# Loads of samples and stores of results issued as two transfers each, 80 rows and the rest

## The chip, the cores and the metric

One Trainium2 chip, one core of it. The metric is device time of one execution in microseconds (us), the median over runs; lower is better.

## The reference

The input x holds 64 samples of 750 time steps with 32 features. Cut to what matters here:

```python
h = tok(x, tok_W, tok_b)          # 92 patches of 16 steps, stride 8, each (512 values) @ W.T + b -> 128
h = h + attn(layernorm(h), ...)   # 8 heads of 64, softmax, heads mixed by an 8x8 matrix, layer norm over heads, values, w_out
h = h + ffn(layernorm(h), ...)    # 8 experts, the top 2 of a softmax gate, and one shared expert
return h                          # (64, 92, 128) float32
```

Everything is float32. The change touches only how x comes in and how h goes out; the arithmetic stays.

## The kernel before, in words

The 64 samples are worked on in 16 groups of 4 (SLOTS = 4, NG = 16). A sample is seen as 93 rows (NP2) of 256 values: one row is one stride of 8 steps times 32 features, and patch p is rows p and p + 1. So a group's samples are one DRAM view of 93 rows x 4 samples x 256 float32 (1 KB contiguous each), and are loaded into the buffer xin, one row of the view per SBUF partition. A group's result is 92 rows (N, the patches) x 4 samples x 128 float32 (512 bytes each), staged in the buffer ostage.

The five engines each run the same hand-written list of steps (`SETUP`, then `ORDER_0`, `STEPS` in a hardware loop, then `TAIL`), each doing its own part of a step and waiting on semaphores for the others. All DMA transfers are issued by SyncE (SP), in its program order, onto one hardware queue:

- first the identity matrix (`ident`), then, once GpSimd has cleared xin, the load of group 0 (`load(0)`, L442);
- then seven transfers counted by `first_loaded` (L467): the token weights tok_W into tok_nat (an alias of the buffer ex, so the trace says ex), biases into vecs, the gate weights;
- then qkv (L468), fifteen constants counted by `consts_loaded` (L470: lng, w_out, lnb, rev, three copies of b2, eight pieces of mixw), and four transfers of expert weights counted by `experts_loaded` (L471 to L474, into an alias of act);
- then `load(G + 2)` each time the step XO of group G + 1 has read xin (so at most one load is under way), and one store in each step OT (L482) once ScalarE has written ostage (L692). At the end SP waits for all stores.

What TensorE does at the start, in the order of `SETUP_START`: step XE (4 transposes of xin; waits for `x_loaded`), XO (4 more), pT (4 transposes of tok_W; waits for all of `first_loaded`), pB (vecs and gate), TK (12 matmuls of 368 columns, the patch embedding; needs xe, xo and the split tok weights), pA0 (waits for qkv), TH, pA1, and VectorE's prepW (L818: waits for qkv and all of `consts_loaded`, then runs L821). Later come pV, pO and, last in the setup, prepE on GpSimd, which waits for the expert weights.

`x_loaded` is counted in units of 16 for each transfer: XE of group g waits for 16 * g + 16 (L591). ScalarE waits with `at_least(act, stored, 16 * g)` before it overwrites ostage for group g, so one store is under way at a time.

Of the kernel before, what the change touches and what calls it, by code (L numbers as in the profile page):

```python
# [16 lines left out]
N = (T - PATCH) // STRIDE + 1  # L17
HEADS, DH = 8, 64
E = 8
SLOTS = 4  # L20
NG = B // SLOTS
# [3 lines left out]
NP2 = N + 1  # L25
# [5 lines left out]
LN_EPS = 1e-5  # L31
N_ROUTE = 18
COPY = 32
COPIES = 3
ROWS_CT = (COPIES - 1) * COPY + E

# [128 lines left out]
def audio_tower(nc, x, tok_W, tok_b, w_qkv, reattn_w, ln_g, ln_b, w_out, b_out, gate_w, w1, b1, w2, b2,  # L165
                sw1, sb1, sw2, sb2, ident_dram, rev_dram, out):
    with ExitStack() as ctx:
# [25 lines left out]
        gate_nat = sb("gate_nat", [E, 128])  # L193
        b2_sb = sb("b2_sb", [2 * COPY + E, 128])
        lng = sb("lng", [128, HEADS])
# [20 lines left out]
        xin = sb("xin", [NS, SLOTS, PAIRS])  # L216
# [62 lines left out]
        ostage = sb("ostage", [N, SLOTS, 128])  # L279
# [11 lines left out]
        x_loaded = sem("x_loaded")  # L291
        stored = sem("stored")
# [48 lines left out]
        def at_least(eng, s, value):  # L341

            if isinstance(value, int) and value <= 0:
                return
            eng.wait_ge(s, value)
# [86 lines left out]
        x_pairs = x_rows[:, 0:NP2 * PAIRS].rearrange("b (p k) -> p b k", p=NP2)  # L432
        out_rows = out.rearrange("b p d -> p b d")
# [5 lines left out]
        @block.sync  # L439
        def _(sp):  # L440
            def load(g):
                sp.dma_start(xin[0:NP2, :, :], x_pairs[:, bass.ds(SLOTS * g, SLOTS), :]).then_inc(x_loaded, 16)  # L442

            first = [
                (tok_nat[:, :, :], tok_W.rearrange("d (k f) -> d k f", k=KT)),
                (vecs[0:8, :], b1), (vecs[8:9, :], sb1.unsqueeze(0)), (vecs[9:10, :], sb2.unsqueeze(0)),
                (vecs[10:11, :], tok_b.unsqueeze(0)), (vecs[11:12, :], b_out.unsqueeze(0)),
                (gate_nat[:, :], gate_w),
            ]
            consts = [  # L450
                (lng[:, :], bass.AP(tensor=ln_g.tensor, offset=0, ap=[[0, 128], [1, HEADS]])),
                (wo_nat[:, :, :], w_out.rearrange("d (k f) -> d k f", k=4)),
                (lnb[:, :], bass.AP(tensor=ln_b.tensor, offset=0, ap=[[0, 128], [1, HEADS]])),
                (rev[:, :, :], rev_dram),
            ]
            for r in range(COPIES):
                consts.append((b2_sb[COPY * r:COPY * r + E, :], b2))

            for h in range(HEADS):
                consts.append((mixw[IC * h:IC * h + IC, :],  # L460
                               bass.AP(tensor=reattn_w.tensor, offset=HEADS * h, ap=[[0, IC], [1, HEADS]])))
            assert len(first) == N_FIRST and len(consts) == N_CONSTS
            sp.dma_start(ident[:, :], ident_dram).then_inc(ident_loaded, 16)
            sp.wait_ge(xin_cleared, 1)
            load(0)
            for dst, src in first:
                sp.dma_start(dst, src).then_inc(first_loaded, 16)  # L467
            sp.dma_start(qkv[:, :, :], w_qkv.rearrange("(c p) d -> p c d", p=128)).then_inc(qkv_loaded, 16)  # L468
            for dst, src in consts:
                sp.dma_start(dst, src).then_inc(consts_loaded, 16)  # L470
            sp.dma_start(w1_sb[:, 0:E, :], w1.rearrange("e h f -> h e f")).then_inc(experts_loaded, 16)  # L471
            sp.dma_start(w1_sb[:, E, :], sw1).then_inc(experts_loaded, 16)
            sp.dma_start(w2_sb[:, 0:E, :], w2.rearrange("e f h -> f e h")).then_inc(experts_loaded, 16)
            sp.dma_start(w2_sb[:, E, :], sw2).then_inc(experts_loaded, 16)  # L474

            def do(step, G):
                if step == "XO" and exists(G + 2, NG):
                    wait_filled(sp, "XO", G)
                    load(G + 2)
                if step == "OT":  # L480
                    wait_emptied(sp, "OT", G)
                    sp.dma_start(out_rows[:, bass.ds(SLOTS * (G - 2), SLOTS), :],  # L482
                                 ostage[:, :, :]).then_inc(stored, 16)

            run(sp, do)
            sp.wait_ge(stored, 16 * NG)

        @block.tensor
        def _(pe):
# [79 lines left out]
            def do(step, G):  # L569
# [11 lines left out]
                g = G + LAG[step]  # L581
# [5 lines left out]
                if step == "XE":  # L587
                    if isinstance(G, int) and G == FIRST:
                        pe.wait_ge(pool_consts, 1)
                        pe.wait_ge(ident_loaded, 16)  # L590
                    pe.wait_ge(x_loaded, 16 * g + 16)  # L591
                if step == "BS":
                    pe.wait_ge(xsum_ready, g + 1)
                if step == "OP":
# [26 lines left out]
                elif step == "TK":  # L621

                    for k in range(KT):
                        rows = [m[:, :, k // 2:k // 2 + N] for m in (xe, xo)[k % 2]]
# [64 lines left out]
        def _(act):  # L689
# [43 lines left out]
            def do(step, G):  # L733
                if isinstance(step, tuple):
                    kind, s = step
                    b = SLOTS * G + s - BEHIND[kind]
                    if kind in ("exa", "exb"):
                        softmax_exp(b, s, int(kind == "exb"))
                    if kind == "ev":
                        act.wait_ge(av_ready, b + 1)  # L740
                        act.activation(oT[0][:, :, (s - 2) % SLOTS, :], values(), ACT.Copy).then_inc(oT_high, 1)
                    if kind == "sq":
                        square(b)
                    if kind == "rstd":
                        attention_rstd(b)
                    return
                g = G + LAG[step]
                if step == "R2":
                    act.wait_ge(route, N_ROUTE * g + 2)
                    act.activation(exl[:, :, :], shift_l[:, :, :], ACT.Exp).then_inc(exl_ready, 1)  # L750
                if step[0] == "H":

                    k = int(step[1])
                    last = f"C{2 * k + 1}" if k < E // 2 else f"Z{E}"
                    wait_emptied(act, last, G)
                    two = slice(2 * k, min(2 * k + 2, E + 1))
                    act.activation(act1_split[0][:, two, :], act1[:, two, :], ACT.Copy).then_inc(units_high, 1)  # L757
                if step in NO_FILL:
                    return
                ps = bank(step)  # L760
                if step in ("XE", "XO"):
                    wait_filled(act, step, G)
                    act.activation((xe if step == "XE" else xo)[0][:, :, :], patches(ps), ACT.Copy)\
                       .then_inc(patch_high, 1)
                elif step == "TK":
                    at_least(act, shifted, G + 1)
                    empty(step, G, hT[:, :, :].rearrange("p s n -> p (s n)"), ps[:, 0:W], func=ACT.Identity,
                          bias=vecT[:, 10:11])
                elif step == "TX":
                    wait_filled(act, step, G)  # L770
                    act.activation(xT_split[0][:, :], ps[:, 0:W], ACT.Copy).then_inc(high_ready[0], 1)  # L771
                elif step == "TX2":
                    wait_filled(act, step, G)
                    act.activation(x2T[0][:, :], ps[:, 0:W], ACT.Copy).then_inc(high_ready[1], 1)
                elif step == "CT":
                    wait_filled(act, step, G)
                    act.activation(combT[0:ROWS_CT, :], ps[0:ROWS_CT, 0:W], ACT.Copy).then_inc(high_ready[2], 1)
                elif step in ("Y0", "Y2", "Y4", "Y6"):
                    empty(step, G, yT[:, :, :, int(step[1]), :], chunked(ps))
                elif step in ("V0", "V2", "V3"):  # L780
                    empty(step, G, v_sb[:, int(step[1]), :], ps[0:N, :])
                elif step[0] == "Z":
                    e = int(step[1])
                    if e == 0:
                        at_least(act, pool_units, len(UNITS_BY_POOL) * g)
                        at_least(act, dve_units, len(UNITS_BY_DVE) * g)
                        if present("YF", G - 1):
                            wait_filled(act, "YF", G - 1)
                    wait_filled(act, step, G)
                    ins = act.activation(act1[:, e, :], ps[:, 0:W], ACT.Relu, bias=vecT[:, e:e + 1])  # L790
                    ins.then_inc(emptied[BANK[step]], 1)
                elif step == "OT":
                    at_least(act, stored, 16 * g)
                    empty(step, G, ostage[:, :, :].rearrange("p s n -> p (s n)"), ps[0:N, :])

            run(act, do, prepare)
# [365 lines left out]
```

## Time and profile before

| what | value |
|---|---|
| time, median of 3 runs | 754.84 us (751.76 to 755.04) |
| the profiled execution: its own time | 750.55 us |
| the profiled execution: span of the trace | 748.8 us |
| mean granted TensorE clock | 0.972 |
| TensorE matmul busy | 685.5 us (92% of the span) |
| VectorE, ScalarE, GpSimd busy | 539.1, 469.1, 352.4 us |
| DMA | 12.03 MB, mean 16 GB/s |
| chain that ended last | PE 78%, DVE 11%, ACT 4%, DMA 1% |

The span runs from the first to the last instruction of the trace; the execution's own time is 1.75 us longer. The profiled execution was 4.29 us below the median of the runs shown. TensorE is busy nearly all the time except in the first and the last of the 40 slices of the span.

### The profile page before, as it was taken

The page shows a single profiled execution, that of the slowest core. Times are in us where ns is not written, and L with a number is a line of the kernel's source. Part 1 is how long each engine was busy: PE and PEld are TensorE (multiplying, and loading weights), DVE is VectorE, ACT ScalarE, POOL GpSimd, SP SyncE. Part 2 cuts the span into 40 slices and gives each one's busy share as a digit, 9 for nine tenths or more (in the row PEclk, how much of TensorE's full clock was granted, in tenths as well). Part 3 has the DMA queues.
Part 4 walks back from the last instruction along what each step waited for, and adds up shares of the span by engine and source line. Part 5 has one row for each costly group of instructions (what it writes and reads, how often), then busy time and mean ns, then how long its engine had stood idle before and what let it go on. Part 6 is the DMA issues. An engine that isn't in the chain of part 4 may idle for free.

```text
span 748.8 us, 16667 instructions
## 1 busy us (share of the span) xinstructions
PE 685.5 (92%) x5238; PEld 620.4 (83%) x5238; DVE 539.1 (72%) x1575; ACT 469.1 (63%) x1494; POOL 352.4 (47%) x435
## 2 busy tenths in 40 slices
PE   2679999999999999999999999999999999998846
PEld 2568889898898989898898989898898989886735
DVE  1755586968777786968777786968777786966544
ACT  1246576685848666685847666685847676675514
POOL 1434336554554536554554536554554536554302
PEclk9899899999999999999999999999999999998968
DMA  3300000000000000000000000000000000000000
GB/s 96 83 22 1 22 3 21 12 17 8 7 19 10 20 10 20 10 17 8 7 19 10 20 10 20 10 16 9 6 20 10 20 10 1 12 1 11 1 10 11
DMA packets 17057, 12.03 MB, mean 16 GB/s; under 512 B 924, under 2 KB 16776, under 8 KB 17032
## 3 DMA queue, kind: packets, MB, share of 16 engines
q1 hardware_dynamic: 17032, 11.71, 5.6%
q8 instruction: 13, 0.21, 0.1%
q14 instruction: 12, 0.10, 0.0%
HBM read 8.70 MB, written 3.01 MB: 16 GB/s over the span
## 4 chain that ended last, share of the span: by engine, by line
PE 78%; DVE 11%; ACT 4%; issue 3%; DMA 1%; POOL 1%; POOLq 0%; DVEq 0%; ACTq 0%
PE ps_fill L337 15%; PE ps_fill L339 13%; PE ps_fill L338 12%; PE ps_dots L542 11%; PE ps_mix L554 11%; PE ps_fill L497 7%; PE ps_av L562 5%; PE ps_fill L664 3%; DMA xin<-in_x 1%; DVE key L937 1%; ACT ex L701 1%; ACT xT_split_hi L771 1%; DVE xT_split_lo L1032 1%; DVE top L939 1%; DVE combine L943 1%
## 5 line engine op out<-in xcount | busy, mean ns | idle before, releaser
L1100 POOL TENSOR_TENSOR sum<-sq 92x384 f32<-92x384 f32 x64 | 64.1, 1001 | 201.7 <-ACT sq L709 201.7
L701 ACT ACTIVATE ex<-ps_dots,negmax 128x92 f32<-128x92 f32 x384 | 123.5, 342 | 38.1 <-DVE negmax L952 38.1
L542 PE MATMUL ps_dots<-xT,yT 128*128 128x96 f32 x768 | 96.4, 275 | 7.6 <-ACT ex L701 4.3
L542 PEld LDWEIGHTS ps_dots<-xT,yT 128*128 128x128 f32 x768 | 91.6, 192 | 11.3 <-issue 10.9
L554 PE MATMUL ps_mix<-mixk,probs 128*92 128x128 f32 x768 | 96.8, 277 | 2.6 <-POOL probs L1094 1.5
L1094 POOL TENSOR_TENSOR probs<-ex,rinv 128x552 f32<-128x552 f32 x64 | 71.0, 1109 | 52.6 <-DVE rinv L958 52.6
L1050 DVE TENSOR_TENSOR act<-ps_fill,act 128x368 f32<-128x368 f32 x128 | 64.5, 534 | 40.7 <-PE ps_fill L664 40.3
L790 ACT ACTIVATE act<-ps_fill,vecT 128x368 f32<-128x368 f32 x144 | 76.5, 566 | 27.3 <-PE ps_fill L339 27.0
L407 POOL TENSOR_TENSOR act_split_lo<-act,act_split_hi 128x736 fp32r<-128x736 f32 (+1 forms) x48 | 81.2, 1706 | 25.0 <-ACT act_split_hi L757 23.8
L554 PEld LDWEIGHTS ps_mix<-mixk,probs 128*92 128x92 f32 x768 | 89.5, 163 | 4.0 <-POOL probs L1094 2.0
L701 ACT ACTIVATION_READ_ACCUMULATOR ex<-ps_dots,negmax 128x1 f32 x384 | 81.6, 212 | 0.0
L971 DVE TENSOR_TENSOR aT<-ps_mix,arstd 92x360 f32<-92x360 f32 x128 | 61.6, 522 | 5.6 <-ACT arstd L719 5.0
L562 PE MATMUL ps_av<-aT,v_sb 92*64 92x96 f32 x1024 | 57.7, 256 | 3.8 <-DVE aT L973 2.3
L709 ACT ACTIVATE sq<-ps_mix 92x768 f32<-92x768 f32 x64 | 52.3, 817 | 10.0 <-PE ps_mix L554 9.9
L757 ACT ACTIVATE act_split_hi<-act 128x736 fp32r<-128x736 f32 (+1 forms) x80 | 57.1, 752 | 0.9 <-DVE act L1050 0.8
L562 PEld LDWEIGHTS ps_av<-aT,v_sb 92*64 92x64 f32 x1024 | 45.5, 139 | 13.6 <-issue 11.1
L337 PE MATMUL ps_fill<-x2T_hi,w_split_hi 128*128 128x368 f32 x144 | 51.7, 359 | 0.7 <-DVE combT L1044 0.7
L407 DVE TENSOR_TENSOR act_split_lo<-act,act_split_hi 128x736 fp32r<-128x736 f32 x32 | 47.9, 1528 | 5.9 <-ACT act_split_hi L757 5.7
L715 ACT ACTIVATE lnvar<-sumsq,eps 92x96 f32<-92x96 f32 x64 | 24.1, 376 | 42.4 <-POOL sumsq L1107 42.3
L337 PE MATMUL ps_fill<-xT_split_hi,A_hi 128*128 128x368 f32 x128 | 47.2, 368 | 3.0 <-DVE yT L802 2.3
L952 DVE TENSOR_REDUCE negmax<-ps_dots 128x6 f32<-128x552 f32 x64 | 46.3, 723 | 3.0 <-PE ps_dots L542 2.9
L337 PE MATMUL ps_fill<-act_split_hi,w_split_hi 128*128 128x368 f32 x144 | 48.4, 336 | 0.0
(169 smaller groups left out, 1772.4 us busy)
## 6 DMA issues: line engine op xcount, KB each, us to landing
xin<-in_x SPq DMA_DIRECT2D x16, 372.0 KB
out<-ostage SPq DMA_DIRECT2D x16, 184.0 KB
act<-in_L_ffn_w SPq DMA_DIRECT2D x2, 512.0 KB, 4.5
qkv<-in_L_attn_w_qkv SPq DMA_DIRECT2D x1, 768.0 KB, 8.1
ex<-in_L_tok_W SPq DMA_DIRECT2D x1, 256.0 KB
ex<-in_L_attn_w_out SPq DMA_DIRECT2D x1, 256.0 KB
mixw<-in_L_attn_reattn_w SPq DMA_DIRECT2D x8, 0.5 KB
act<-in_L_ffn_sw SPq DMA_DIRECT2D x2, 64.0 KB, 4.3
```

The source lines that it names most:

```text
L337: nc.tensor.matmul(out, s_hi, m_hi, start=start, stop=False)
L338: nc.tensor.matmul(out, s_hi, m_lo, start=False, stop=False)
L339: return nc.tensor.matmul(out, s_lo, m_hi, start=False, stop=stop)
L407: eng.tensor_tensor(lo, act1[:, two, :], hi.bitcast(F32), ALU.subtract).then_inc(done, 1)
L542: last = pe.matmul(ps_dots[:, c // HALF, o:o + NS], yT[:, 2 * s + c // HALF, c % HALF, :, :].rearrange("p h i -> p (h i)"), xT[:, N * s:N ...
L554: last = pe.matmul(ps_mix[0:N, c // HALF, o:o + 128], probs[:, (s - 1) % 2, c, :], mixk[:, :, :].rearrange("p g i -> p (g i)"), start=True ...
L562: last = pe.matmul(ps_av[o:o + DH, NS * (g // 2):NS * (g // 2) + NS], v_sb[:, (s - 2) % SLOTS, DH * g:DH * g + DH], aT[:, s % 2, N * g:N * ...
L701: last = act.activation(ex[:, s % 2, c, :], ps_dots[:, c // HALF, o:o + N], ACT.Exp, bias=negmax[:, c:c + 1], accum_out=sums[:, s % 2, c:c ...
L790: ins = act.activation(act1[:, e, :], ps[:, 0:W], ACT.Relu, bias=vecT[:, e:e + 1])
L1050: ins = dve.tensor_tensor(act1[:, e, :], ps[:, 0:W], act1[:, e, :], ALU.mult)
L1094: pool.tensor_tensor(probs[:, s % 2, :, :], ex[:, s % 2, :, :], rinv[:, s % 2, :].unsqueeze(2).broadcast_to([128, CHUNKS, N]), ALU.mult).t ...
L1100: pool.tensor_tensor(sum4[:, :, :, :], sq[:, :, 0:4, :], sq[:, :, 4:8, :], ALU.add)\
```

## The change

Each load of samples becomes two transfers, rows 0 to 79 and rows 80 to 92 of the same view; each store becomes two, rows 0 to 79 and 80 to 91. Both transfers of a pair add 16 to the same semaphore, so what waits for them counts in units of 32.

```diff
+SPREAD_ROWS = 80
...
             def load(g):
-                sp.dma_start(xin[0:NP2, :, :], x_pairs[:, bass.ds(SLOTS * g, SLOTS), :]).then_inc(x_loaded, 16)
+                for rows in (slice(0, SPREAD_ROWS), slice(SPREAD_ROWS, NP2)):
+                    sp.dma_start(xin[rows, :, :], x_pairs[rows, bass.ds(SLOTS * g, SLOTS), :]).then_inc(x_loaded, 16)
...
                 if step == "OT":
                     wait_emptied(sp, "OT", G)
-                    sp.dma_start(out_rows[:, bass.ds(SLOTS * (G - 2), SLOTS), :],
-                                 ostage[:, :, :]).then_inc(stored, 16)
+                    for rows in (slice(0, SPREAD_ROWS), slice(SPREAD_ROWS, N)):
+                        sp.dma_start(out_rows[rows, bass.ds(SLOTS * (G - 2), SLOTS), :],
+                                     ostage[rows, :, :]).then_inc(stored, 16)
...
-            sp.wait_ge(stored, 16 * NG)
+            sp.wait_ge(stored, 32 * NG)
...
-                    pe.wait_ge(x_loaded, 16 * g + 16)
+                    pe.wait_ge(x_loaded, 32 * g + 32)
...
-                    at_least(act, stored, 16 * g)
+                    at_least(act, stored, 32 * g)
```

## Rows read from the trace of the kernel before

**Rows 1.** The page: granted TensorE clock in tenths, 40 slices of the span

```profile
PEclk9899899999999999999999999999999999998968
```

**Rows 2.** Chain that ended last, in order of time: start, length, what

```profile
1.72 10.76 DMA xin<-in_x
...
12.61 2.38 PE ps_fill L497 x12
```

**Rows 3.** Timeline of the first 40 us: start, length, engine, line, what

```profile
1.72 0.31 SPq L442 DMA_DIRECT2D xin<-in_x  x1
2.08 2.02 SPq L467 DMA_DIRECT2D ex<-in_L_tok_W  x1
...
4.14 1.50 SPq L467 DMA_DIRECT2D vecs<-in_L_ffn_b  x1
...
6.86 0.27 SPq L467 DMA_DIRECT2D gate_nat<-in_L_ffn_gate_w  x1
7.18 0.40 SPq L468 DMA_DIRECT2D qkv<-in_L_attn_w_qkv  x1
7.62 3.51 SPq L470 DMA_DIRECT2D lng<-in_L_attn_ln_g  x1
...
13.76 0.82 PEld L497 LDWEIGHTS ps_fill<-ident,ex 128*128 128x128 f32 x4
...
14.04 3.55 SPq L470 DMA_DIRECT2D mixw<-in_L_attn_reattn_w  x8
...
17.63 0.42 SPq L471 DMA_DIRECT2D act<-in_L_ffn_w  x1
...
20.37 1.46 PEld L523 LDWEIGHTS ps_fill<-qkv 64*128 64x128 f32 x8 [0.41 <-issue]
...
25.08 1.38 DVE L821 TENSOR_TENSOR probs<-qkv,lng 64x512 f32<-64x512 f32 x2
```

**Rows 4.** The page's DMA issues: transfers, KB each, median us from issue to landing

```profile
qkv<-in_L_attn_w_qkv SPq DMA_DIRECT2D x1, 768.0 KB, 8.1
...
ident<-const_ident SPq DMA_DIRECT2D x1, 64.0 KB, 1.9
```

**Rows 5.** Stretches of 1 us while load 0 and the weights come in; last two columns: DMA share, GB/s

```profile
3.00:4.00 1.00, 0.00 (x0) 0.00 (x0) 0.00 (x0) 0.00 (x0) 0.76 (x7) 1.00 0.23 12
...
5.00:6.00 1.00, 0.00 (x0) 0.00 (x0) 0.00 (x0) 0.00 (x0) 0.00 (x0) 1.00 0.75 241
...
7.00:8.00 1.00, 0.00 (x0) 0.00 (x0) 0.00 (x0) 0.00 (x0) 0.00 (x0) 1.00 0.21 68
...
20.00:21.00 1.00, 1.00 (x5) 0.63 (x4) 0.00 (x0) 0.46 (x1) 0.00 (x0) 1.00 1.14 345
```

**Rows 6.** The same for a load alone (first and last of 7 rows, and one between)

```profile
44.00:45.00 1.00, 0.00 (x0) 0.00 (x0) 0.81 (x2) 0.60 (x4) 0.00 (x0) 1.00 0.14 25
...
48.00:49.00 1.00, 1.00 (x11) 1.00 (x10) 0.73 (x1) 0.08 (x1) 0.42 (x1) 1.00 0.22 74
...
50.00:51.00 1.00, 1.00 (x8) 1.00 (x7) 0.00 (x0) 1.00 (x4) 0.25 (x1) 1.00 0.14 45
```

**Rows 7.** The same for the last store (last two of 3 rows)

```profile
746.00:747.00 1.00, 0.00 (x0) 0.00 (x0) 0.00 (x0) 0.00 (x0) 0.00 (x0) 0.50 0.27 76
747.00:748.00 1.00, 0.00 (x0) 0.00 (x0) 0.00 (x0) 0.00 (x0) 0.00 (x0) 0.50 0.24 73
```

**Rows 8.** Waits of the DMA queue's engine SP: us in total, times, longest

```profile
SPq L167 <- DMA out<-ostage: 3.5, 1, 3.5
```

**Rows 9.** SP's timeline in the loop

```profile
161.63 0.27 SPq L442 DMA_DIRECT2D xin<-in_x  x1
...
203.76 0.25 SPq L442 DMA_DIRECT2D xin<-in_x  x1
```

**Rows 10.** Stretches of 2 us where the clock fell; the third last column is the clock

```profile
76.00:78.00 2.00, 1.05 (x14) 1.08 (x16) 1.47 (x4) 0.00 (x0) 0.04 (x1) 0.51 0.04 8
...
82.00:84.00 2.00, 2.00 (x14) 2.00 (x14) 0.65 (x2) 2.00 (x13) 0.00 (x0) 0.78 0.14 34
```

## The prediction

> **What bounds the kernel now.** I read the views from the whole to the place of the change. The page says TensorE is busy 92% of the span, at full granted clock in most slices [rows 1], and the chain that ended last is 78% TensorE and 1% DMA. So in the loop the transfers can matter little, and the question is whether the 1% is a place where nothing else covers them. The chain in order of time [rows 2] shows it: from 1.72 to 12.48 us it consists of one transfer, load 0, and TensorE's first work (12 transposes: XE, XO, pT) starts at 12.61. The view of SP's waits shows the second place: at the very end SP sits 3.5 us on the last store [rows 8]. Everything between is covered: in the loop SP issues one load per iteration of 203.76 - 161.63 = 42.13 us [rows 9], just after XO has read xin, and the next XE comes most of an iteration later; ostage has the same slack.
>
> **How wide a transfer is now.** A load with nothing beside it (load 2) moves its 372 KB between about 44.3 and 50.7 us; inside that stretch the mean busy share of the 16 DMA engines is 0.22, at 74 GB/s, and over its seven rows it is 1.29 engine-spans, that is 20.6 engine-us [rows 6]. 0.22 x 16 is 3.5, near three engines for 93 rows. The store shows 0.27 and 0.24, four engines, at 73 to 76 GB/s [rows 7], for 92 rows. While 128-row transfers come in, the share is 0.75 to 1.14 at 241 to 345 GB/s [rows 5]. The numbers fit equal shares: 93 = 3 x 31 on 3 engines, 92 = 4 x 23 on 4, 128 = 16 x 8 on 16. With the same reading 80 rows = 16 x 5 use all 16, the remaining 13 and 12 rows use 13 and 12.
>
> The Trainium skill says this as a rule (DMA: Bandwidth & Descriptors, "Why a DMA increments its semaphore by 16 and not by 1"): the number of engines is the largest up to 16 that divides the slowest dimension. By that rule too it is 3 and 4 now and 16, 13 and 12 after; the trace agrees, with its shares of 0.22 and 0.24 to 0.27.
>
> **The change, step 1: the transfer itself.** A load is 372 packets of 1 KB (93 rows x 4), 124 on each of 3 engines; 20.6 engine-us / 372 = 55 ns each. After, an engine has at most 5 x 4 + 4 = 24: 1.3 us where it was 6.4 to 6.9. A store is 368 packets of 512 bytes, 92 on each of 4 engines; 188 kB at 76 and 73 GB/s is 2.5 us, or 27 ns each, 30 ns with the ragged first row. After: 24 x 30 = 0.7 us. Both rates are within what 16 engines have shown (381 kB in 1.3 us is 293 GB/s, 188 kB in 0.7 us is 269, against 345 [rows 5]).
>
> **Step 2: the extra instruction.** SP issues one more transfer per load and store, 0.25 to 0.31 us each [rows 3, 9]. In the loop SP is idle between issues, so it costs nothing; if every one of the 32 lay on the path it would be 32 x 0.28 = 9 us, but then SP would have to be the one that is waited for, and it issues for about 0.5 us in an iteration of 42.13. At the start it delays what is queued behind load 0 by 0.3 us; at the end it overlaps the first part's transfer.
>
> **Step 3: the start.** XE alone isn't what counts: pT waits for all seven `first_loaded` transfers, which stand behind load 0 in the same queue and on the same engines. Its weight loads start at 13.76 [rows 3], right after XO. So I ask when the seventh has landed after the change. SP's issue times show it held up behind load 0: tok_W takes 2.02 us to issue, the next 1.50, lng (after qkv) 3.51, whereas w1, with twice tok_W's bytes, takes 0.42 and small ones 0.27 [rows 3]. What holds it isn't named by the trace; the nearest explanation is the backlog of 124 packets on three engines, since load 0 is the only narrow large transfer and SP runs freely again after it has drained.
> - If the hold goes: 1.72 + 2 x 0.33 for load 0, 0.42 for tok_W, five small ones, the last issued at about 4.3; the identity took 1.9 us to land [rows 4], so 6.2. pT at 6.3: gain 7.4 us.
> - If the hold stays as it is: gate_nat issued at 6.86 + 0.3 = 7.2, landed 9.1, pT at 9.2: gain 4.5 us.
> - Between 3 and 4 us the queue moved only 12 GB/s at a share of 0.23 [rows 5]: the first reads are slow, and this may remain. So I lean from the upper end: landed about 7.6, **gain 6.0 us**.
>
> Load 0 itself, with its data moving by 4 to 4.5 us, is in by about 5.5 to 6 and XE and XO (1.2 us) are done before pT, so they aren't the limit.
>
> Is the gain passed on? TK follows pT through ScalarE's and VectorE's split of the tok weights, all compute. Next, pA0 needs qkv at 20.37 - 6.0 = 14.4; qkv landed 8.1 us after 7.18, at 15.3 [rows 3, 4], but with three engines clogged. After, it is issued by 4.7 to 7.5 and its 786 kB at 241 to 345 GB/s need 2.3 to 3.3 us: in by about 12 at the latest. prepW (L821) needs all constants at 25.08 - 6.0 = 19.1; the eight mixw issues ended at 17.6 [rows 3], landing about 19.5. With SP's hold gone they end near 13 and are hidden; with it kept they land at 19.8 while L821 would stand at 25.08 - 4.5 = 20.6, hidden again. The expert weights, issued just behind from 17.63 on [rows 3], are used last in the setup, and come earlier with all the rest. So the 6.0 us go through.
>
> **Step 4: the end.** Of SP's 3.5 us [rows 8] some 2.6 to 2.8 are data moving (about 745.2 to 747.9, [rows 7]) and 0.7 to 0.9 latency. The latency stays; the moving becomes 0.7, or 0.9 if the second part trails by its 0.29 us of issue. Gain between 1.3 (if 16 engines writing at once reach only half the rate per engine) and 2.1; I take **1.9 us**.
>
> **Step 5: the loop.** A load or store now occupies all engines for about a microsecond rather than a few for 3 to 7. Nobody waits for either before or after; I cost it at 0.
>
> **The sum.** 6.0 + 1.9 = 7.9 us. The profiled execution took 750.55 us, so the same execution would take 742.6; it was 4.3 us under the median of the runs shown. On the median: 754.84 - 7.9 = **747 us**.
>
> **The rivals.**
> - *The slow beginning isn't the width.* If first reads of memory set the pace (the 12 GB/s between 3 and 4 us [rows 5] speak for it, the 68 GB/s at a share of 0.21 between 7 and 8 against it), load 0 lands near 8 and pT starts near 10: gain 3.7 + 1.5 = 5.2, time 749.6 us.
> - *The split doesn't spread.* If both parts run on few engines, or side by side at the old total rate, nothing is gained and two issues are paid, 0.3 us at the start and 0.3 at the end: 755.4 us. Against it stand the shares of 128-row transfers in the same queue [rows 5].
> - *The head start is given back in the setup,* at a constant that lands late or at a lower clock: 2 to 3.5 us left, 752 us. For it speaks that L821's inputs have little over a microsecond of margin.
> - *Slower, through the clock.* The granted clock halves after a pause of TensorE: it was low from about 76 to 83 us [rows 10], with TensorE busy nearly throughout, which costs at most half, 3.4 us. An earlier start changes when the pauses of the setup fall. It decides from four more such stretches: 7.9 - 4 x 3.4 = -5.7, time 760.5 us. Rows 1 show only two slices below 9 ahead of the last four, and the later pauses are the same compute waits, so this is unlikely.
>
> The Trainium skill has a rule that speaks against this change (DMA: Bandwidth & Descriptors, "Rules for kernel authors"): two transfers to disjoint groups of partitions aren't worth it, since both halves use all 16 engines anyway and serialize. By that rule the second rival would hold; its premise, that the single transfer already uses 16 engines, isn't what this trace shows for 93 and 92 rows (0.22 and 0.27).
>
> **How the numbers follow.** My forecast (gain 6 to 9.5, own range 745 to 749) has 0.63; the slow beginning 0.17; no spread 0.05; given back 0.09; slower by the clock 0.04; 0.02 for more than 9.5. The runs shown differ by 3.3 us among themselves, so I widen for the baseline: 743 to 751.5, which leaves out the second, third and fourth rival. About 0.5%, 3.8 us, is what a measurement here can tell from no change. Faster by more: the forecast, the slow beginning and the remainder, 0.82; within: no spread and given back, 0.14; slower: 0.04.
>
> **What would show it.** In the profile after: TensorE's first transposes at 6 to 7 us and pT's at 7 to 8; a loop load at a DMA share near 1 for about 1.5 us; tok_W issued in well under 1 us; SP's last wait 1.6 us rather than 3.5; L821 at about 19; from 40 us on the same pattern, 6 us earlier. The prediction is wrong if the seven transfers land after 10 us, if L821 waits for constants, or if stretches at half clock appear that rows 1 don't have.

## The result, and the profile after

| | kernel before | changed kernel |
|---|---|---|
| median | 751.18 us (749.71 to 755.04, 6 runs) | 744.05 us (740.95 to 744.41, 6 runs) |
| profiled execution: time, span | 750.55, 748.8 us | 744.14, 742.3 us |
| mean granted clock | 0.972 | 0.973 |

The ratio over all these runs is 0.9888 with a 95% interval of 0.9855 to 0.9920: the change made the kernel faster by 1.1%. (The quotient of the two medians is 0.9905, inside that interval.) The six runs of before hold the three that the forecast was made from (median 754.84) and three more, 749.7 to 750.6.

Read first the chain of the changed kernel in order of time, which answers to [rows 2]:

```profile
2.10 3.51 DMA xin<-in_x
5.74 2.51 PE ps_fill L500 x12
```

Load 0 still opens the chain, with 3.51 us rather than 10.76 (counted here from the second of its two issues; from the first, at 1.71, it is 3.9 us), and TensorE starts at 5.74 rather than 12.61. pT, used from here on, is the start of that step's first weight load. The timeline of the same stretch answers to [rows 3]:

```profile
1.71 0.87 SPq L444 DMA_DIRECT2D xin<-in_x  x2
2.62 0.35 SPq L469 DMA_DIRECT2D ex<-in_L_tok_W  x1
3.02 0.34 SPq L469 DMA_DIRECT2D vecs<-in_L_ffn_b  x1
...
5.32 0.69 SPq L472 DMA_DIRECT2D lng<-in_L_attn_ln_g  x1
7.12 0.72 PEld L500 LDWEIGHTS ps_fill<-ident,ex 128*128 128x128 f32 x4 [0.16 <-DMA gate_nat<-in_L_ffn_gate_w]
...
17.75 1.38 DVE L824 TENSOR_TENSOR probs<-qkv,lng 64x512 f32<-64x512 f32 x2
```

SP's three long issues have gone: tok_W 2.02 to 0.35 us, the next 1.50 to 0.34, lng 3.51 to 0.69. pT stands at 7.12, after a wait of 0.16 us for the last of its seven transfers. L824 (L821 before) stands at 17.75 rather than 25.08.

Stretches of 1 us (DMA share and GB/s last): load 0, load 3 in the loop, and the last store, against [rows 5 to 7]:

```profile
3.00:4.00 1.00, 0.00 (x0) 0.00 (x0) 0.00 (x0) 0.00 (x0) 0.75 (x7) 1.00 0.91 291
...
76.00:77.00 1.00, 1.00 (x9) 0.85 (x8) 0.89 (x2) 1.00 (x8) 0.00 (x0) 1.00 0.56 127
77.00:78.00 1.00, 1.00 (x8) 1.00 (x7) 0.00 (x0) 1.00 (x9) 0.00 (x0) 1.00 0.88 254
...
740.00:741.00 1.00, 0.00 (x0) 0.00 (x0) 0.00 (x0) 0.00 (x0) 0.00 (x0) 0.71 0.46 113
741.00:742.00 1.00, 0.00 (x0) 0.00 (x0) 0.00 (x0) 0.00 (x0) 0.00 (x0) 0.50 0.30 75
```

Between 3 and 4 us, where 12 GB/s moved, 291 GB/s now move: the slow start went with the narrow load. Its three engines alone don't explain it, since the same share gave 68 GB/s between 7 and 8 us; what held them at 12 isn't shown. The loop's load takes two rows with shares of 0.56 and 0.88, 1.44 x 16 = 23 engine-us, near the 20.6 of before, but spread. The last store's two rows add up to 0.76 x 16 = 12 engine-us; taken by tenths of a microsecond, its share stands at 0.9 from 740.6 to 741.1. SP's waits, against [rows 8]:

```profile
SPq L168 <- DMA out<-ostage: 1.4, 1, 1.4
```

and SP's timeline at the end, the last store's two issues:

```profile
739.65 0.80 SPq L485 DMA_DIRECT2D out<-ostage  x2
```

In the trace of before that issue stood at 744.66 and took 0.26. So the span is shorter by 744.66 - 739.65 = 5.0 us up to the last store and by (748.8 - 744.66) - (742.3 - 739.65) = 1.5 us behind it, 6.5 in all, though pT came 6.6 us earlier and L824 7.3. Between the setup and the last store, 2.3 us were lost again. VectorE's score maxima (L955, L952 before; the maximum that each softmax subtracts) show where: the first stands at 36.32 (before 43.64, 7.3 us earlier), the third at 48.63 (before 54.31, 5.7 us earlier). So 1.6 us go between these two; 0.1 more go until the load issued at 577.36 (582.92 before), and 0.6 behind it. Granted clock of the changed kernel in that stretch (third last column):

```profile
40.00:41.00 1.00, 1.00 (x10) 1.00 (x9) 0.22 (x2) 0.00 (x0) 1.00 (x3) 0.84 0.08 16
41.00:42.00 1.00, 1.00 (x6) 1.00 (x6) 0.57 (x1) 0.40 (x3) 0.10 (x1) 0.50 0.02 8
42.00:43.00 1.00, 1.00 (x6) 1.00 (x6) 0.00 (x0) 0.67 (x5) 0.00 (x0) 0.50 0.00 0
```

The next row is the same, and about 44 us the clock is back. TensorE is busy throughout, at the 1.2 GHz level: six matmuls in a microsecond. Before that it had stood still for 2.8 us, up to 39.25, while ScalarE made the first exponentials. The trace of before has the same pause of 2.8 us, up to 46.56, and no low stretch behind it. Whether that belongs to the change was the first question for the experiments.

The theory that they test: **a transfer is as wide as its row count lets it be; of 32 transfers only load 0 and the last store lie on the path; what moves beside that is where the granted clock falls.** The rivals: two transfers are better than one wherever they are cut; the loop's transfers matter; SP's long issues have a cause other than load 0; the low stretch after the setup comes with the change.

### The profile page after: what moved, and what is told of

It is laid out like the page before. It is cut to its first block, busy times and chain, and to the rows that moved or that the text cites. A ratio compares the mean times of both kernels' runs of the same rounds, so it can differ in the third digit from the quotient of the medians.

```text
span 742.3 us, 16747 instructions
## 1 busy us (share of the span) xinstructions
PE 686.9 (93%) x5238; PEld 621.7 (84%) x5238; DVE 538.5 (73%) x1575; ACT 469.8 (63%) x1494; POOL 352.3 (47%) x435
## 4 chain that ended last, share of the span: by engine, by line
PE 80%; DVE 11%; ACT 4%; issue 3%; POOL 1%; DMA 0%; SPq 0%; DVEq 0%; POOLq 0%; ACTq 0%
PE ps_fill L338 15%; PE ps_fill L339 13%; PE ps_fill L340 13%; PE ps_dots L545 11%; PE ps_mix L557 11%; PE ps_fill L500 7%; PE ps_av L565 5%; PE ps_fill L667 4%; DVE key L940 1%; ACT xT_split_hi L774 1%; DVE xT_split_lo L1035 1%; DVE top L942 1%; ACT ex L704 1%; DVE combine L946 1%; DVE yT L805 1%
## 5 line engine op out<-in xcount | busy, mean ns | idle before, releaser
L955 DVE TENSOR_REDUCE negmax<-ps_dots 128x6 f32<-128x552 f32 x64 | 46.2, 722 | 3.1 <-PE ps_dots L545 2.9
```

## Experiments

**The two halves of the change.** Loads alone, then stores alone, and the changed kernel again on the same chip.

```diff
 # e1_loads_only: the store as before, and its waits in units of 16
-                    for rows in (slice(0, SPREAD_ROWS), slice(SPREAD_ROWS, N)):
-                        sp.dma_start(out_rows[rows, ...], ostage[rows, :, :]).then_inc(stored, 16)
+                    sp.dma_start(out_rows[:, ...], ostage[:, :, :]).then_inc(stored, 16)
```

> Only the loads are split (80 + 13 rows); the stores stay whole. Theory (each transfer is limited by how many DMA engines its row count lets it use, and only load 0 and the last store lie on the path): pT's first weight load at about 7.1 us as in the changed kernel (13.8 before), SP's last wait back at 3.5 us; time about 1.5 us above the changed kernel and about 5 us under the kernel before. Rival (splitting stores matters in the loop, or split loads disturb it): the distance between loop loads departs from 42.1 us.

```diff
 # e2_stores_only: the load as before, and its wait in units of 16
-                for rows in (slice(0, SPREAD_ROWS), slice(SPREAD_ROWS, NP2)):
-                    sp.dma_start(xin[rows, :, :], x_pairs[rows, ...]).then_inc(x_loaded, 16)
+                sp.dma_start(xin[0:NP2, :, :], x_pairs[:, ...]).then_inc(x_loaded, 16)
```

> Only the stores are split (80 + 12 rows); the loads stay whole. Theory: pT at 13.8 us as before, SP's last wait 1.4 us rather than 3.5; the second part's issue costs 0.5 us of that, so the time falls by 1.5 us, not to be told from no change with certainty. Rival (all of the gain is at the start): no change of the last stretch, 0.0 us.

> The changed kernel once more, on the same chip as the others of this call. Theory: ratio to the kernel before 0.989 to 0.992, pT at 7.1 us. It is the yardstick for the other three.

| kernel | median | ratio to before, 95% | pT | last store's issue to the end of the span |
|---|---|---|---|---|
| before (23 runs) | 752.08 us | | 13.76 us | 4.14 us |
| e1_loads_only | 743.78 | 0.9882 (0.9843 to 0.9921) | 7.21 | 742.1 - 738.03 = 4.07 |
| e2_stores_only | 750.89 | 0.9975 (0.9947 to 1.0002) | 13.54 | 748.4 - 745.79 = 2.61 |
| e3_changed_again | 744.05 | 0.9869 (0.9833 to 0.9905) | 7.29 | 740.7 - 738.05 = 2.65 |

(pT and the last column are from each kernel's trace.) The traces add up: the loads bring pT, the stores 1.5 us at the end. In the times the loads' part is clear and the stores' 1.2 us is not, as expected. Two numbers were missed: e1 was to be 5 us under the kernel before and was 8.3 under it, and it was to be 1.5 us above the changed kernel and came out 0.3 under e3. The second is within the spread of the runs. So that the split of the stores shortens the time is seen in the traces, and not shown by the times.

e3's trace bears on the question of the clock. Its granted clock from 41 us on:

```profile
41.00:42.00 1.00, 1.00 (x11) 1.00 (x11) 0.43 (x1) 0.00 (x0) 0.84 (x3) 1.00 0.02 8
42.00:43.00 1.00, 1.00 (x11) 1.00 (x10) 0.30 (x1) 0.66 (x5) 0.00 (x0) 1.00 0.00 0
```

The same program, the same stretch, eleven matmuls in a microsecond: no low level. Its third score maximum stands at 47.73 and its last store at 738.05. pT gained 13.76 - 7.29 = 6.5 us, and the last store comes 744.66 - 738.05 = 6.6 us earlier. Its later low stretches, too, lie where those of the trace of before do, 6 to 7 us earlier (for one, 69 to 76 us against 76 to 83). Where the clock falls as before, the head start goes through whole.

**Two transfers, cut where it doesn't help.**

```diff
-                for rows in (slice(0, SPREAD_ROWS), slice(SPREAD_ROWS, NP2)):
+                for rows in (slice(0, 69), slice(69, NP2)):       # 69 and 24 rows
...
-                    for rows in (slice(0, SPREAD_ROWS), slice(SPREAD_ROWS, N)):
+                    for rows in (slice(0, 46), slice(46, N)):     # 46 and 46 rows
```

> Two transfers each as in the changed kernel, but cut where the row counts have few divisors: loads 69 + 24 rows (69 = 3 x 23 on 3 engines, 24 = 2 x 12 on 12), stores 46 + 46 (2 engines each, by the reading of equal shares). Theory: a low engine of a load then carries 23 x 4 + 2 x 4 = 100 packets rather than 124 (24 in the changed kernel), so load 0 is only a fifth faster: pT near 11.5 to 12.5 us; a store has 92 x 2 = 184 packets on each of 2 engines, 5 us or more: SP's last wait 5.5 to 6.5 us. Time about that of the kernel before, plus or minus 1.5 us. Rival (two transfers are faster than one because there are two, wherever the cut is): as the changed kernel, pT near 7.1 us and a last wait near 1.4 us.

Measured: 752.87 us, ratio 1.0009 (0.9981 to 1.0036); nothing gained. Its last store in stretches of 1 us, and SP's wait for it:

```profile
748.00:749.00 1.00, 0.00 (x0) 0.00 (x0) 0.00 (x0) 0.00 (x0) 0.00 (x0) 0.50 0.14 37
749.00:750.00 1.00, 0.00 (x0) 0.00 (x0) 0.00 (x0) 0.00 (x0) 0.00 (x0) 0.50 0.12 25
```

```profile
SPq L168 <- DMA out<-ostage: 6.0, 1, 6.0
```

0.12 to 0.14 of 16 engines is two for both parts together, as 46 = 2 x 23 says, and the wait grew from 3.5 to 6.0 us. At the store two narrow transfers are worse than one, and at the load pT came 4 us behind the changed kernel's, so the rival falls. pT came at 11.10, a little ahead of what was expected and 2.7 us ahead of before; yet L824 stands at 24.07, only 1.0 us earlier than before. The timeline shows where the other 1.7 went:

```profile
17.70 2.07 PE L526 MATMUL ps_fill<-qkv 64*128 64x128 f32 x8
...
20.72 2.07 PE L526 MATMUL ps_fill<-qkv 64*128 64x128 f32 x8
```

In the changed kernel's trace both groups take 1.16 us:

```profile
13.54 1.16 PE L526 MATMUL ps_fill<-qkv 64*128 64x128 f32 x8
```

In the trace of before the first takes 1.66 and the second 1.16. e4 did the same work at the low level, in a stretch that in the other traces was at the high one, at the latest from the second group on.

**Only load 0.**

```diff
-                for rows in (slice(0, SPREAD_ROWS), slice(SPREAD_ROWS, NP2)):
+                pieces = (slice(0, SPREAD_ROWS), slice(SPREAD_ROWS, NP2)) if isinstance(g, int) and g == 0 else (slice(0, NP2),)
+                for rows in pieces:
...
-                    pe.wait_ge(x_loaded, 32 * g + 32)
+                    pe.wait_ge(x_loaded, 16 * g + 32)             # and the stores whole, as in e1
```

> Only load 0 is split (80 + 13 rows); the fifteen other loads and all stores stay whole. Theory (only load 0 lies on the path): pT at 7.1 to 7.3 us, SP's last wait 3.5 us, time as with all loads split (743.8 us there, 744 to 745 here). Rival (the loop's loads give something or cost something): off that by a multiple of 15, so that even 0.1 us each would show as 1.5 us.

Measured: 744.55 us, ratio 0.9901 (0.9877 to 0.9925), pT at 7.00 us, last wait 3.5 us. With fifteen loads and all stores whole the time is within 1 us of the others. The interval is 1.8 us to either side, so 0.1 us for each load would not have shown in the time. The traces settle it: ten iterations of the loop take 582.92 - 161.63 = 421.29 us before, 577.36 - 155.98 = 421.38 us in the changed kernel and 577.03 - 155.71 = 421.32 us here. The loop's transfers give nothing and cost nothing.

**What held SP.** The kernel before, load 0 moved behind the seven transfers that pT waits for.

```diff
-            load(0)
             for dst, src in first:
                 sp.dma_start(dst, src).then_inc(first_loaded, 16)
+            load(0)
```

> The kernel before (one transfer each), with load 0 issued behind the seven transfers that pT waits for rather than ahead of them. Theory (what held SP at tok_W, 2.02 us, was the backlog of load 0's 124 packets on three engines): tok_W is issued in about 0.35 us, gate_nat by 3.7 us; load 0 is issued at about 4 us and lands near 11.5 to 12.5 us; then the first transposes come at 11 to 12.5 us rather than 12.6, and lng behind load 0 and qkv is still held by 3 us. Time 0 to 1.5 us under the kernel before. Rival (SP's hold comes from the first transfers of a program, or from the 512 packets of tok_W itself): tok_W takes 2 us here too.

Measured: 753.67 us, ratio 1.0033 (1.0016 to 1.0051), slower by 0.3%. SP's timeline:

```profile
1.71 0.36 SPq L466 DMA_DIRECT2D ex<-in_L_tok_W  x1
...
4.00 0.27 SPq L442 DMA_DIRECT2D xin<-in_x  x1
6.06 6.75 SPq L470 DMA_DIRECT2D lng<-in_L_attn_ln_g  x1
14.33 1.25 PEld L497 LDWEIGHTS ps_fill<-ident,xin 96*128 96x128 f32 x8 [14.33 <-issue]
```

Without load 0 ahead of it tok_W is issued in 0.36 us, so it was load 0 that held SP, and behind load 0 the hold is back: 1.70 us at qkv and 6.75 at lng. That part of the theory stands. The rest was missed: load 0 landed at 14.2, not 11.5 to 12.5, and the time is 1.8 us above the kernel before rather than 0 to 1.5 under it. Load 0 took 10.2 us here and 10.8 in the kernel before, where a whole load in the loop takes about 7.5 from issue to the end of its data. It was slow beside the other transfers both times; how a narrow transfer shares its engines with wide ones isn't settled by these traces.

Three more traces bear on the hold. In the kernel before profiled again (b1 and b2 below) lng took 5.16 and 6.64 us to issue, so its length varies from one execution to the next. In e4, behind 69 and 24 rows, tok_W was issued in 0.36 us and only lng was held, for 3.03: by equal shares the fullest engine has 100 packets there rather than 124, which speaks for the amount of the backlog and not for the three engines as such. And the hold cost the kernel before nothing that shows: in b1 gate_nat was issued at 5.56 rather than 6.86, and pT stands at 13.74 against 13.76, right behind XO both times. What pT waited for was load 0 itself.

**A later start.** Cleared in another order, so that xin is free 1.0 us later.

```diff
-            pool.memset(xin[:, :, :], 0.0).then_inc(xin_cleared, 1)
             pool.memset(minus_half[:, :], -0.5)
             for tile in xn:
                 pool.memset(tile[:, :, :], 0.0)
+            pool.memset(xin[:, :, :], 0.0).then_inc(xin_cleared, 1)
```

> The changed kernel, with GpSimd's clearing of minus_half and xn (about 1.0 us) moved ahead of that of xin, for which load 0 waits. So load 0 starts 1.0 us later, and nothing else is changed. Theory: pT at 8.1 us, time plus 1.0 us, but the stretch of half clock after 40 us, which cost the changed kernel's trace 1.6 us and its second trace nothing, may come or not: +0 to +2.6 us. Rival (there is slack between load 0 and the end of the setup): no change.

Measured: 744.28 us, ratio 0.9905 (0.9881 to 0.9929), pT at 7.99 (+0.87), first score maximum at 37.17 (+0.85), last store at 740.39 (+0.74), low stretch at 41 to 44 us present. The delay goes through to the end in the trace. In the time, 0.2 us above the 744.05 measured on other chips, it can't be told from no change.

**tok_W ahead of load 0**, as the version that might beat the change:

```diff
+            sp.dma_start(*first[0]).then_inc(tok_loaded, 16)      # tok_W
             sp.wait_ge(xin_cleared, 1)
             load(0)
-            for dst, src in first:
+            for dst, src in first[1:]:
...
-                    pe.wait_ge(first_loaded, 16 * N_FIRST)        # pT
+                    pe.wait_ge(tok_loaded, 16)                    # and pB waits for the six others
```

> The changed kernel with tok_W issued ahead of load 0, in the 0.6 us in which SP waits for xin to be cleared, and with pT waiting for tok_W alone (pB for the six small ones). Theory: pT follows XO without a wait; load 0 lands a little later (0.2 us), so pT moves by 0.0 to 0.3 us: no difference that can be measured, at most 0.3 us. Rival (something of the seven small transfers still holds the start by more than the 0.16 us of wait in the changed kernel's trace): a gain of over 1 us.

Measured: 743.90 us, ratio 0.9901 (0.9880 to 0.9923), pT at 7.34 us. Load 0 lands 0.4 us later for tok_W's sake and pT no longer waits for its own inputs: nothing won. None of these versions beats the changed kernel by more than the spread of the runs.

**Is the low stretch the change's?** Both kernels unedited, profiled twice more.

> The kernel before, profiled once more. Theory (where the granted clock falls is chance from one execution to the next of the same kernel, and moves the end by 1 to 3 us): the last store's issue at 743 to 748 us, with a low stretch at 46 to 50 us or without; pT stays at 13.5 to 13.9 us. Rival (the low stretch after 40 us belongs to the changed kernel): none there in either trace of the kernel before.

> The kernel before a second time, with the same expectation: pT at 13.5 to 13.9 us, the last store's issue at 743 to 748 us, where it falls to be set by the stretches of low clock.

> The changed kernel, profiled once more. Theory: pT at 7.1 to 7.3 us, SP's last wait 1.4 to 1.5 us; the last store's issue at 738.05 us where the stretch of low clock at 40 to 44 us is absent, 739.6 where it is there. Rival (the 1.6 us between the two earlier traces has another cause): one of the two times without its pattern.

> The changed kernel a second time, with the same expectation: the last store's issue at 738.05 us without the stretch of low clock at 40 to 44 us, at 739.6 with it.

| trace | pT | low stretch just after the setup | third score maximum | last store's issue |
|---|---|---|---|---|
| before | 13.76 | none | 54.31 | 744.66 |
| b1_before_again | 13.74 | 47 to 50 us | 55.13 | 745.93 |
| b2_before_again | 15.06 | none | 55.34 | 745.66 |
| changed | 7.12 | 40 to 44 us | 48.63 | 739.65 |
| a1_changed_again | 7.05 | 39 to 43 us | 48.13 | 738.92 |
| a2_changed_again | 6.97 | 40 to 44 us | 48.54 | 739.49 |
| e3_changed_again | 7.29 | none | 47.73 | 738.05 |

Each kernel shows it in some executions and not in others, so it doesn't belong to the change; that rival falls. Its price can be read inside each trace: from L824 (L821 before) to the third score maximum it is 29.2 us without the stretch and 30.8 to 30.9 with it, in all fourteen traces of this document. So it costs 1.6 us. At the last store the traces of the changed kernel with it stand 0.9, 1.4 and 1.6 us behind e3: their L824 came 0.7 to 1.2 us ahead of e3's, and the later low stretches differ as well (a1's next one lasts from 70 to 77 us as in e3, that of the changed kernel's first trace only from 71 to 74). So a1 missed its expectation: 738.92 where 739.6 was expected.

It isn't spread at random either. It came in all seven traces in which the first eight qkv matmuls already took 1.16 us (the changed kernel's first, a1, a2, e2, e5, e7, b1), and in none of the six in which they took 1.40 to 1.74 (before, b2, e1, e3, e6, e9). e4, with 2.07 us for both groups, had it too. So it goes with how the clock stood in the setup; why is not shown.

b2's pT, expected at 13.5 to 13.9, came at 15.06: load 0 itself landed 1.0 us later than in the other two, which the wide version hasn't shown (6.97 to 7.29 in four traces). Times were 751.82 and 751.56 us before, 743.38 and 743.98 changed, one run each.

## Where the prediction was right, and the step that failed

- *Step 1, the width.* Right. 93 rows on 3 engines and 92 on 4 became transfers over all 16: a load with shares of 0.56 and 0.88 for under 2 us, a store that reaches 0.9. e4 supports the arithmetic: 46 rows give two engines. How wide the parts of 13 and 12 rows run was not seen apart. The Trainium skill's rule (DMA: Bandwidth & Descriptors, "Why a DMA increments its semaphore by 16 and not by 1") is borne out by e4's share of 0.12 to 0.14. The Trainium skill's rule against two transfers to disjoint partition halves (DMA: Bandwidth & Descriptors, "Rules for kernel authors") rests on both using all 16 engines anyway. It did not hold for 93 and 92 rows, whose single transfer used 3 and 4 engines (shares of 0.22 and 0.24 to 0.27).
- *Step 2, the extra instruction.* Mis-sized: a pair takes 0.87 us at the load and 0.80 at the store from the first issue's start, where 0.6 was reckoned from issues of 0.25 to 0.31. It is hidden in the loop. At the end it is on the path, and at the start it lies ahead of load 0's landing; what it costs there was not measured apart.
- *Step 3, the start.* The mechanism is right and the size a little low: gain 6.6 us against 6.0. The upper bound's reason held (SP's hold was load 0's backlog, as e6 shows for tok_W). It was wrong that XE and XO "aren't the limit": they and the seventh transfer end together. pT waited 0.16 to 0.17 us for that transfer in two of the four traces of the changed kernel and not at all in the other two. In the kernel before the limit was load 0 alone. The margin of L821 was real, and nothing waited there. In the changed kernel's first trace L824 came 7.3 us earlier, not 6.6, since the first qkv matmuls already ran in 1.16 us; in e3's, with 1.63 us, it was 6.6.
- *Step 4, the end.* SP's wait fell by 2.1 us, of which the longer pair of issues took 0.5: 1.5 us against 1.9. The second issue's 0.54 us where 0.29 was reckoned makes 0.25 of the missing 0.4; the rest is not resolved.
- *Step 5, the loop.* Right: 421.38 against 421.29 us for ten iterations.
- *The rival of the clock* was priced and given 0.04 as a way to be slower; four more low stretches didn't come. But one did in three of four traces of the changed kernel, as in one of three of the kernel before, at 1.6 us. So the same pattern 6 us earlier, forecast for the stretch from 40 us on, was wrong in those three. It is also one of the prediction's own signs of being wrong, a low stretch that the kernel before didn't have in its trace. (The mean granted clock doesn't show it: 0.972 before, 0.973 after.) In the first trace of the changed kernel this accounts for the 5.0 us at the last store: 6.6 at pT, 0.7 more by L824, 1.6 lost in the stretch, 0.1 in the loop and 0.6 behind it.
- *The sum.* 7.9 us were forecast. Between medians it was 751.18 - 744.05 = 7.1, between the traces 6.5, from the trace of before to e3's, where the clock falls alike, 748.8 - 740.7 = 8.1. That 7.9 came so near 8.1 is in part luck: the start gave 0.6 more and the end 0.4 less than forecast.
- *The step that failed* is the last one, "On the median: 754.84 - 7.9". The term that was mis-sized is the time of the kernel before. The median of three runs, 754.84, stood for it; six runs gave 751.18, and the 23 and 16 of the experiments 752.08 and 751.87 us (747.87 to 757.67), 3 us lower. So the forecast of 747, with its own range of 745 to 749, lies 3 us above the 744.05 measured, though the saving was right. 752.08 - 7.9 = 744.2 would have met it. The profiled execution, 750.55 - 7.9 = 742.6, was nearer than the median of three, and the text had put it aside.

## What to carry to other kernels

Look at the DMA share while one transfer runs alone. Here 0.22 and 0.24 to 0.27 of 16 engines went with 93 and 92 rows, whose divisors up to 16 are poor, and cutting them at 80, a multiple of 16, brought a load's data from 6.4 to under 2 us. It pays only where something waits for that transfer, which here was once at the start and once at the end. A narrow transfer at the head of a queue also holds up the issue of what stands behind it. Here that cost nothing that shows, since what waited was waiting for the load itself (b1 against before). And where a forecast is a time and not a ratio, the base is a term of it like any other: three runs put it 3 us too high, for a saving of 8.

## What the runs showed that was not expected

- A transfer's issue isn't always 0.25 us: behind load 0 on three engines SP needed 2.02, 1.50 and 3.51 us for single issues, up to 6.64 in another trace of the same kernel, and 6.75 us in e6.
- The clock column says 1.00 over the first 17 us of every trace, and in the trace of before up to 24 us, while the matmuls of 368 columns there follow each other every 0.31 us, 368 / 0.307 = 1.2 GHz. In that stretch the spacing has to be read, not the column. The same pause of TensorE of 2.8 us sometimes had the low level behind it and sometimes not, in the same program.
